# Linear attention stage with a rewritten scalar order and a freed LayerNorm bank, and a 4-bit FFN stage with a reordered TensorE order

## The chip, the cores and the metric

The kernel is written directly against the five engines of a NeuronCore of a Trainium2 chip: TensorE (PE), VectorE (DVE), ScalarE (ACT), GpSimd (POOL) and SyncE (SP). It runs on one core. Every engine has its own program and runs it strictly in the order written; the programs meet at semaphores. The metric is the device time of one execution in microseconds, as the median of several runs.

## What is computed

The reference is a chain of twelve stages on an activation `x` of 16 sequences x 256 tokens x 128 channels, all fp32. Four blocks follow one another, each of the form "half an FFN, attention, half an FFN": ffn0, attn0, ffn0, ffn1, attn1, ffn1, ffn2, attn2, ffn2, ffn3, attn3, ffn3. Each stage normalises `x` over the channels and adds its result to `x`. The change touches two of the stage types.

attn1 is eight layers of linear attention with an MLP (H*K = 1024 = 8 blocks of 128 rows, MLP width F = 512 = 4 blocks):

```python
for i in range(8):
    residual = x
    Q  = elu(x @ Wq[i] + bq[i]) + 1
    Kf = elu(x @ Wk[i] + bk[i]) + 1
    V  = x @ Wv[i] + bv[i]
    KV, sumK = sum_over_tokens(Kf * V), sum_over_tokens(Kf)
    att = Q * KV * (1 / (Q * sumK + 1e-6))
    y = gelu(att @ Wo[i] + bo[i])
    x = layer_norm(y + residual) * s1 + b1
    residual = x
    h = gelu(x @ W1[i] + c1[i])
    h = gelu(h @ W2[i] + c2[i])
    x = layer_norm(h + residual) * s2 + b2
```

ffn3 (which runs twice) quantises to 4-bit floats and back, in blocks of 16 along the last dimension:

```python
h = silu(fp4(x) @ fp4(w_gate).T) * (fp4(x) @ fp4(w_up).T)     # 352 columns
out = fp4(h) @ fp4(w_down).T
```

## The kernel before

**Tiling.** The 4096 tokens are taken in G = 8 groups of GT = 512 tokens (QT = 4 tiles of 128). All of `x` stays in SBUF. PSUM is one tensor `bank` of 8 banks of 128 x 512 fp32. Scratch of every stage lies in one SBUF tensor, `arena`, so most rows of the profile name only `arena` and `bank` and must be told apart by their lines.

**Software pipeline.** A stage is a list of parts (lag, function) for each engine. Slot s calls each part for group s - lag, in the order of the list. `over_groups` runs the 8 slots of an ordinary stage and the slots of its tail. `over_layers` runs attn1: eight layers of eight slots, 64 in all, and 3 slots of tail; group g of layer l + 1 starts where group 7 of layer l has only begun, so that the pipeline does not drain between layers. The loop over the layers is a loop on the chip, at whose edge every engine branches.

**attn1.** `steps(layer)` writes the four lists by hand. It goes through w = 0..7, the eight blocks of 128 rows of a projection. The lists before, for PE, block by block (lag in brackets):

- w0: `proj_pe(0)` [0], `turn_in_pe(0)` [2], `h2_pe(2)` [3], `out_pe(4)` [1]
- w1: `proj_pe(1)`, `h2_pe(3)` [3], `out_pe(5)` [1]
- w2: `proj_pe(2)`, `turn_back_pe(0)` [2], `out_pe(6)` [1]
- w3: `proj_pe(3)`, `out_pe(7)` [1]
- w4: `proj_pe(4)`, `h_pe` of MLP block 0 [2]
- w5: `proj_pe(5)`, `h_pe` of MLP blocks 1, 2, 3 [2], `turn_in_pe(1)` [3], `out_pe(0)`, `out_pe(1)`
- w6: `proj_pe(6)`, `turn_back_pe(1)` [3], `h2_pe(0)` [2], `out_pe(2)`
- w7: `proj_pe(7)`, `h2_pe(1)` [2], `out_pe(3)`

`proj_pe(i)` (L1805) makes three 128 x 512 products, k, q and v of block i, into a ring of five banks (`RING1` = 2, 3, 4, 5, 7); product m waits until product m - 5 has been read. Each fp32 product is two passes of TensorE, so it shows as two MATMULs. `out_pe` (L1820) accumulates att @ Wo in bank 6. `h_pe` (L1849) makes the four blocks of the MLP's inner layer in banks `HBANK` = (0, 1, 6, 0). `h2_pe` (L1859) accumulates the second MLP product in bank 1. `turn_in_pe(i)` (L1876) and `turn_back_pe(i)` (L1885) are the four 128 x 128 transposes into and out of token-major form that LayerNorm i (0 or 1) needs; both use bank 0.

ACT, block by block: `exp_act(w)` (L1896 exp of k, L1897 relu of k, L1900 exp of q), then `inv_act` (L1909 Ln, L1912 Exp), of block w - 2, except that w4 has none and w5 has blocks 2 and 3. After `norm_act(0)` (L2034) in w1 and `back_act(0)` (L1952) in w2 comes the gelu phase in w4: load the gelu table (L1917), `h2_act` (L1939, reads bank 1), `y_act` (L1923, reads bank 6), `h_act` for the four MLP blocks (L1932), load the exp table (L1943). `norm_act(1)` (L2034) ends w5, `back_act(1)` (L1956) ends w6.

DVE, block by block: `feature_dve(w)` (L1968 to L1986; it reads the q and v banks), `att_dve(w - 3)` (L2009), with `norm_stats_dve(0)` (L2020, L2025) at the end of w0 and `norm_stats_dve(1)` at the end of w4. POOL: `query_pool(w)` (L2046), `ratio_pool(w)` (L1997), the residual additions and the rstd of both LayerNorms (L2068 to L2075) after the stats.

**ffn3.** DVE, per slot: `stats_dve` [0], `apply_dve` [1], `quant_x_dve` [1], `quant_h_dve` [2], `add_dve` (L852) [3]. The quantisation is `fp4_steps`, ten DVE instructions (L705 to L714), on 512 elements per partition for x and on 1408 for h. `quant_h_dve` first makes four products silu x up (L811), each for one tile q of 352 columns, straight from the PSUM bank. PE: `transpose_pe` (L784) [0], `down_pe` (L831 transposes, L837 products) [1], `up_pe` (L794 gate, L795 up) [0]; `up_pe` for tile q waits until L811 has read the banks of tile q - 2. ACT: `copy_act` (L336) [0], `copy_h_act` (L847) [1], `silu_act` (L804) [0].

Of the kernel before, what the change touches and what calls it, by code (L numbers as in the profile page):

```python
# [10 lines left out]
ALU = mybir.AluOpType  # L11
# [3 lines left out]
P = 128  # L15
# [23 lines left out]

ARENA = 28320  # L40

# [127 lines left out]
def macaron(nc, A, out, stages=STAGES):  # L169
    ctx = ExitStack()  # L170
    with ctx:
# [546 lines left out]
        if "ffn3" in used:  # L718
# [18 lines left out]
            f3_h = scratch("f3_h", [P, QT, FF3])  # L737
            f3_silu = scratch("f3_silu", [P, 2, FF3])
            f3_xq = scratch("f3_xq", [P, 2, QT, D])
# [5 lines left out]
            f3_up = ev("f3_up", per=QT)  # L745
            f3_act = ev("f3_act", per=QT)
            f3_mul = ev("f3_mul", per=QT, credit=2, by="vector")
            f3_turned = ev("f3_turned", per=len(F3B), credit=2 * len(F3B), by="tensor")
# [16 lines left out]
        def ffn3(n, rep):  # L765
# [21 lines left out]
            def up_pe(g, u):  # L787
                s = g + rep * G
                xt_ready.wait(nc.tensor, g + n * G)
                if n and isinstance(g, int) and g == 0:  # L790
                    x_written.wait(nc.tensor, n * G - 1)
                for q in range(QT):
                    f3_mul.wait_free(nc.tensor, s, q + 1)
                    nc.tensor.matmul(bank[:, 2 + 2 * (q % 2), 0:FF3], xT_tile(u, q), wgT[:], start=True, stop=True)  # L794
                    nc.tensor.matmul(bank[:, 3 + 2 * (q % 2), 0:FF3], xT_tile(u, q), wuT[:], start=True, stop=True)\  # L795
                        .then_inc(f3_up.sem, 1)

            def silu_act(g, u):
                s = g + rep * G
                if n and isinstance(g, int) and g == 0:  # L800
                    x_written.wait(nc.scalar, n * G - 1)
                for q in range(QT):
                    f3_up.wait(nc.scalar, s, q + 1)
                    nc.scalar.activation(f3_silu[:, q % 2, :], bank[:, 2 + 2 * (q % 2), 0:FF3], ACT.Silu)\  # L804
                        .then_inc(f3_act.sem, 1)

            def quant_h_dve(g, u):
                s = g + rep * G
                for q in range(QT):
                    f3_act.wait(nc.vector, s, q + 1)  # L810
                    nc.vector.tensor_tensor(f3_h[:, q, :], f3_silu[:, q % 2, :], bank[:, 3 + 2 * (q % 2), 0:FF3],  # L811
                                            ALU.mult).then_inc(f3_mul.sem, 1)
                f3_mul.wait(nc.vector, s)
# [36 lines left out]
            def add_dve(g, u):  # L850
# [7 lines left out]
            programs["tensor"].append(lambda e: over_groups(  # L858
                e, [(0, transpose_pe), (1, down_pe), (0, up_pe)], gate(e, n)))
            programs["scalar"].append(lambda e: over_groups(  # L860
                e, [(0, copy_act), (1, copy_h_act), (0, silu_act)], gate(e, n)))


# [785 lines left out]
        if "attn1" in used:  # L1649
# [76 lines left out]
            RING1 = (2, 3, 4, 5, 7)  # L1726
            HBANK = (0, 1, 6, 0)

        def attn1(n, rep):
# [54 lines left out]
            def steps(layer):  # L1784
# [5 lines left out]

                def proj_pe(i):
                    def fn(g, u):
# [5 lines left out]
                        if i % 4 == 0 and isinstance(g, int):  # L1798
                            nc.tensor.wait_ge((a1_half0, a1_half1)[i // 4], 48 * (layer + 1))
                        for j, k in enumerate("kqv"):  # L1800
                            m = 3 * i + j

# [28 lines left out]
                def h_pe(blocks):  # L1831
                    def fn(g, u):
                        t = turn(g)
                        for i in blocks:
# [12 lines left out]
                            if i == 3:  # L1847
                                a1_h_act.wait(nc.tensor, t, 1)
                            nc.tensor.matmul(bank[:, HBANK[i], :], w1a[:, i * P:(i + 1) * P], a1_x1[:, u, :],  # L1849
# [15 lines left out]
                def turn_in_pe(i):  # L1865
                    def fn(g, u):
                        t = turn(g)
                        lns[i]["in"].wait(nc.tensor, t)
                        if i == 0:
                            a1_zt.wait(nc.tensor, t - 2)  # L1870
                            if first_layer and g + 2 < G:
                                xt_ready.wait(nc.tensor, n * G + g + 2)
                        elif not (isinstance(g, int) and g == G - 1):
                            a1_h_act.wait(nc.tensor, t + 1)
                        for q in range(QT):
# [209 lines left out]
                for w in range(NB1):  # L2085
                    pe.append((0, proj_pe(w)))
                    if w == 0:
# [9 lines left out]
                    if w == 5:  # L2097
                        pe += [(2, h_pe((1, 2, 3))), (3, turn_in_pe(1))]
                        of(pe, out_pe, 0)
                    if w == 6:  # L2100
                        pe += [(3, turn_back_pe(1)), (2, h2_pe(0))]
                    if w == 7:
                        pe.append((2, h2_pe(1)))
                    if w != 4:
# [5 lines left out]
                    if w == 5:  # L2110
                        of(act, inv_act, 2)
                    if w != 4:
                        of(act, inv_act, w - 2)
                    if w == 1:
                        act.append((2, norm_act(0)))
                    if w == 2:
                        act.append((2, back_act(0)))
                    if w == 5:
                        act.append((3, norm_act(1)))
                    if w == 3 and first_layer:  # L2120
                        act.append((-1, first_act))
                    if w == 6:
                        act.append((3, back_act(1)))

                    dve.append((0, feature_dve(w)))
# [816 lines left out]
```

## Time and profile before

| what | value |
|---|---|
| time, median of 3 runs (lowest to highest) | 5036.86 us (5023.66 to 5044.8) |
| the profiled execution | 5024.43 us, of which the span of the core's instructions is 5022.6 us |
| PE busy | 4048.0 us, 81% of the span |
| DVE busy | 3528.2 us, 70% |
| ACT busy | 3069.5 us, 61% |
| POOL busy | 1550.1 us, 31% |
| attn1's 64 slots of projections | 746.8 to 3363.9 us |
| the two ffn3 stages | about 3835 to 4078 and 4786 to 5023 us |

The page also cuts the span into 40 slices and gives the busy tenths of every engine:

```profile
PE   4487759999989999998998999983877549999944
...
DVE  4588569877777777777777777765657745666576
ACT  1355328888888888888888888881221115565511
...
PEclk9678679999999999999999999996998669999976
```

A digit is the busy share of a slice of 125.6 us in tenths; PEclk is TensorE's granted clock in tenths of full speed. The long stretch of nines and eights from the seventh slice on is attn1. The last slices of each row are the second ffn3.

### The profile page before, as it was taken

The page shows a single profiled execution, that of the slowest core. Times are in us where ns is not written, and L with a number is a line of the kernel's source. Part 1 is how long each engine was busy: PE and PEld are TensorE (multiplying, and loading weights), DVE is VectorE, ACT ScalarE, POOL GpSimd, SP SyncE. Part 2 cuts the span into 40 slices and gives each one's busy share as a digit, 9 for nine tenths or more (in the row PEclk, how much of TensorE's full clock was granted, in tenths as well). Part 3 has the DMA queues.
Part 4 walks back from the last instruction along what each step waited for, and adds up shares of the span by engine and source line. Part 5 has one row for each costly group of instructions (what it writes and reads, how often), then busy time and mean ns, then how long its engine had stood idle before and what let it go on. Part 6 is the DMA issues. An engine that isn't in the chain of part 4 may idle for free.

```text
span 5022.6 us, 66047 instructions
## 1 busy us (share of the span) xinstructions
PE 4048.0 (81%) x15980; PEld 2267.0 (45%) x15980; DVE 3528.2 (70%) x11356; ACT 3069.5 (61%) x5586; POOL 1550.1 (31%) x2846
## 2 busy tenths in 40 slices
PE   4487759999989999998998999983877549999944
PEld 2265633444444444443443444432554436676633
DVE  4588569877777777777777777765657745666576
ACT  1355328888888888888888888881221115565511
POOL 1222124444434444343443443432100023333300
PEclk9678679999999999999999999996998669999976
DMA  1011010000000000000000000000000001111000
GB/s 52 17 32 22 15 21 1 1 20 3 12 12 1 18 5 1 20 3 14 9 1 18 5 6 17 1 1 0 0 0 0 0 22 42 40 40 39 26 0 17
DMA packets 132031, 69.71 MB, mean 14 GB/s; under 512 B 92345, under 2 KB 124814, under 8 KB 129316
## 3 DMA queue, kind: packets, MB, share of 16 engines
q1 hardware_dynamic: 124020, 52.62, 4.3%
q10 hardware_dynamic: 7600, 12.58, 0.7%
q8 instruction: 139, 2.28, 0.2%
q14 instruction: 272, 2.23, 0.1%
HBM read 52.39 MB, written 12.80 MB: 13 GB/s over the span
## 4 chain that ended last, share of the span: by engine, by line
PE 46%; DVE 19%; ACT 15%; issue 11%; POOL 4%; DMA 3%; ACTq 1%; SPq 1%; DVEq 0%; POOLq 0%
PE bank L1805 11%; PE bank L1849 4%; PE bank L1820 4%; PE bank L2574 3%; ACT arena L2034 3%; ACT arena L1909 3%; PE bank L1859 3%; DVE arena L2009 2%; DMA packed_dram<-arena 2%; DVE arena L1986 2%; ACT arena L1897 2%; PE bank L2607 2%; ACT arena L1900 2%; PE bank L643 2%; ACT arena L1896 2%
## 5 line engine op out<-in xcount | busy, mean ns | idle before, releaser
L1805 PE MATMUL bank<-arena 128*128 128x512 f32 x3072 | 1411.0, 596 | 12.1 <-issue 11.8
L1805 PEld LDWEIGHTS bank<-arena 128*128 128x128 f32 x3072 | 588.7, 192 | 761.5 <-issue 749.2
L2046 POOL TENSOR_SCALAR arena<-arena 128x256 f32<-128x256 f32 x1024 | 496.0, 494 | 1215.9 <-DVE arena L1979 1214.8
L1968 DVE SCALAR_TENSOR_TENSOR arena<-arena 128x256 f32<-128x256 f32 x1024 | 393.1, 420 | 303.1 <-ACT arena L1897 303.0
L1820 PE MATMUL bank<-arena 128*128 128x512 f32 x1024 | 537.4, 617 | 39.1 <-DVE arena L2009 38.9
L2009 DVE SCALAR_TENSOR_TENSOR arena<-arena 128x256 f32<-128x256 f32 x1024 | 528.3, 554 | 0.0
L1896 ACT ACTIVATE arena<-bank,bqk 128x512 f32<-128x512 f32 x512 | 351.9, 687 | 221.6 <-PE bank L1805 189.4
L1986 DVE SCALAR_TENSOR_TENSOR arena<-bank,bv,arena 128x256 f32<-128x256 f32 x1024 | 444.7, 472 | 0.0
L1979 DVE SCALAR_TENSOR_TENSOR arena<-bank,bq,arena 128x512 f32<-128x512 f32 x512 | 384.0, 750 | 18.0
L1909 ACT ACTIVATE arena<-arena,const_table 128x512 f32<-128x512 f32 x512 | 374.9, 732 | 0.0
L2585 DVE TENSOR_REDUCE arena<-bank 128x2 f32<-128x512 f32 x256 | 176.2, 688 | 258.5 <-PE bank L2576 258.3
L1900 ACT ACTIVATE arena<-bank,bqk 128x512 f32<-128x512 f32 x512 | 355.9, 695 | 0.7 <-PE bank L1805 0.7
L1897 ACT ACTIVATE arena<-bank,bqk 128x512 f32<-128x512 f32 x512 | 351.5, 686 | 0.0
L1912 ACT ACTIVATE arena<-arena 128x512 f32<-128x512 f32 x512 | 322.5, 630 | 16.3
L2561 POOL TENSOR_TENSOR arena<-arena 128x256 f32<-128x256 f32 x256 | 185.9, 726 | 439.7 <-DVE arena L2551 439.1
L2618 ACT ACTIVATE arena<-bank 128x512 f32<-128x512 f32 x256 | 153.3, 599 | 269.9 <-PE bank L2607 211.1
L2574 PE MATMUL bank<-const_table,arena 128*128 128x256 f32 x1024 | 310.7, 397 | 3.5 <-POOL arena L2561 3.5
L2020 DVE BATCH_NORM_STATS2 arena<-bank 128x6 f32<-128x128 f32 x512 | 113.1, 280 | 280.3 <-PE bank L1876 280.3
L1820 PEld LDWEIGHTS bank<-arena 128*128 128x128 f32 x1024 | 185.5, 197 | 260.1 <-issue 160.7
L1859 PE MATMUL bank<-arena 128*128 128x512 f32 x512 | 284.8, 642 | 0.0
L313 POOL TENSOR_SCALAR rstd<-meanvar 128x4 f32<-128x4 f32 x96 | 20.5, 213 | 782.0 <-DVE meanvar L307 731.8
L1849 PE MATMUL bank<-arena 128*128 128x512 f32 x512 | 244.5, 601 | 1.0 <-ACT arena L1952 1.0
(371 smaller groups left out, 7577.8 us busy)
## 6 DMA issues: line engine op xcount, KB each, us to landing
arena<-packed_dram SPq DMA_DIRECT2D x48, 192.0 KB
arena<-packed_dram ACTq DMA_DIRECT2D x16, 576.0 KB
arena<-diag_dram SPq DMA_DIRECT2D x16, 256.0 KB, 3.9
arena<-in_L_attn_Wk_dram SPq DMA_DIRECT2D x16, 256.0 KB, 3.2
arena<-in_L_attn_Wq_dram SPq DMA_DIRECT2D x16, 256.0 KB, 4.0
arena<-in_L_attn_Wv_dram SPq DMA_DIRECT2D x16, 256.0 KB, 4.4
arena<-in_L_attn_Wo_dram SPq DMA_DIRECT2D x8, 512.0 KB, 3.8
arena<-in_L_attn_W_dram SPq DMA_DIRECT2D x16, 256.0 KB, 2.7
```

What stands on the lines that cost most here:

```text
L1805: nc.tensor.matmul(bank[:, RING1[m % 5], :], w1p[k][:, i * P:(i + 1) * P], zT_of(g), start=True, stop=True).then_inc(a1_proj.sem, 1)
L1820: nc.tensor.matmul(bank[:, 6, :], wo1[:, i, :], a1_att[:, i % 4, :], start=(i == 0), stop=(i == NB1 - 1)).then_inc(a1_outd.sem, 1)
L1849: nc.tensor.matmul(bank[:, HBANK[i], :], w1a[:, i * P:(i + 1) * P], a1_x1[:, u, :], start=True, stop=True).then_inc(a1_h_psum.sem, 1)
L1859: one = nc.tensor.matmul(bank[:, 1, :], w1b[:, i, :], a1_h[:, i, :], start=(i == 0), stop=(i == NF1 - 1))
L1896: nc.scalar.activation(a1_ek[:, i % 4, :], k, ACT.Exp, bias=bqk[:, 0, i:i + 1])
L1897: nc.scalar.activation(a1_kf[:, i % 4, :], k, ACT.Relu, bias=bqk[:, 0, i:i + 1])\
L1900: nc.scalar.activation(a1_eq[:, i % 4, :], q, ACT.Exp, bias=bqk[:, 1, i:i + 1])\
L1909: nc.scalar.activation(a1_z[:, i % 4, :], a1_qf[:, i % 4, :], ACT.Ln, bias=table[:, C_TINY:C_TINY + 1]).then_inc(a1_ln.sem, 1)
L1986: last = nc.vector.scalar_tensor_tensor(seqs(a1_ek[:, i % 4, :])[q], seqs(b[2])[q], bv1[:, i:i + 1], seqs(a1_kf[:, i % 4, :])[q], ALU.add, ...
L2009: last = nc.vector.scalar_tensor_tensor(seqs(a1_att[:, i % 4, :])[q], seqs(a1_qf[:, i % 4, :])[q], a1_kv[:, i % 4, q:q + 1], seqs(a1_z[:, ...
L2046: last = nc.gpsimd.tensor_scalar(a, a, 1.0, a1_ksum[:, i % 4, b:b + 1], ALU.add, ALU.mult)
L2574: nc.tensor.matmul(dst, a3_R[:, w % 4, i * P:(i + 1) * P], table[:, C_KEYS:C_KEYS + T], start=True, stop=False)
```

## The change

In attn1: (a) MLP block 3 goes into bank 1 and no longer into bank 0, its product now waits for the gelu of MLP block 1 (before: of block 0), and `turn_in_pe(1)` waits for the gelu of MLP block 0 alone (before: of all four). (b) `proj_pe(5)` is split: k, then MLP blocks 1 to 3, then q and v, then `turn_in_pe(1)`. (c) `turn_back_pe(1)` moves from behind the products of w6 to behind those of w7. (d) On ACT, `inv_act(3)` moves from w5 to w6, behind `exp_act(6)`; `norm_act(1)` follows it, ahead of `inv_act(4)`; `back_act(1)` moves to w7, ahead of `inv_act(5)`.

In ffn3: (e) PE and ACT do the up products and their silu ahead of the down products of the group before. (f) ACT copies the up product out of PSUM beside the silu, for all four tiles, into double buffers; PE waits for ACT's copy and not for DVE. (g) DVE multiplies silu x up in one instruction of 1408 elements. The arena is 64 elements per partition smaller.

```diff
@@ -37,7 +37,7 @@
 
-ARENA = 28320
+ARENA = 28256
 
@@ -735,7 +735,8 @@
     f3_h = scratch("f3_h", [P, QT, FF3])
-    f3_silu = scratch("f3_silu", [P, 2, FF3])
+    f3_silu = scratch("f3_silu", [P, 2, QT, FF3])
+    f3_upc = scratch("f3_upc", [P, 2, QT, FF3])
     f3_xq = scratch("f3_xq", [P, 2, QT, D])
@@ -743,8 +744,8 @@
     f3_up = ev("f3_up", per=QT)
-    f3_act = ev("f3_act", per=QT)
-    f3_mul = ev("f3_mul", per=QT, credit=2, by="vector")
+    f3_act = ev("f3_act", per=QT, credit=2, by="scalar")
+    f3_mul = ev("f3_mul", credit=2, by="vector")
     f3_turned = ev("f3_turned", per=len(F3B), credit=2 * len(F3B), by="tensor")
@@ -790,7 +791,7 @@
         for q in range(QT):
-            f3_mul.wait_free(nc.tensor, s, q + 1)
+            f3_act.wait_free(nc.tensor, s, q + 1)
             nc.tensor.matmul(bank[:, 2 + 2 * (q % 2), 0:FF3], xT_tile(u, q), wgT[:], start=True, stop=True)
@@ -799,17 +800,18 @@
             x_written.wait(nc.scalar, n * G - 1)
+        f3_mul.wait_free(nc.scalar, s)
         for q in range(QT):
             f3_up.wait(nc.scalar, s, q + 1)
-            nc.scalar.activation(f3_silu[:, q % 2, :], bank[:, 2 + 2 * (q % 2), 0:FF3], ACT.Silu)\
+            nc.scalar.activation(f3_silu[:, u, q, :], bank[:, 2 + 2 * (q % 2), 0:FF3], ACT.Silu)
+            nc.scalar.activation(f3_upc[:, u, q, :], bank[:, 3 + 2 * (q % 2), 0:FF3], ACT.Copy)\
                 .then_inc(f3_act.sem, 1)
...
         s = g + rep * G
-        for q in range(QT):
-            f3_act.wait(nc.vector, s, q + 1)
-            nc.vector.tensor_tensor(f3_h[:, q, :], f3_silu[:, q % 2, :], bank[:, 3 + 2 * (q % 2), 0:FF3],
-                                    ALU.mult).then_inc(f3_mul.sem, 1)
+        f3_act.wait(nc.vector, s)
+        nc.vector.tensor_tensor(f3_h[:], f3_silu[:, u, :, :], f3_upc[:, u, :, :], ALU.mult)\
+            .then_inc(f3_mul.sem, 1)
         f3_mul.wait(nc.vector, s)
@@ -856,9 +858,9 @@
     programs["tensor"].append(lambda e: over_groups(
-        e, [(0, transpose_pe), (1, down_pe), (0, up_pe)], gate(e, n)))
+        e, [(0, transpose_pe), (0, up_pe), (1, down_pe)], gate(e, n)))
     programs["scalar"].append(lambda e: over_groups(
-        e, [(0, copy_act), (1, copy_h_act), (0, silu_act)], gate(e, n)))
+        e, [(0, copy_act), (0, silu_act), (1, copy_h_act)], gate(e, n)))
 
@@ -1724,7 +1726,7 @@
     RING1 = (2, 3, 4, 5, 7)
-    HBANK = (0, 1, 6, 0)
+    HBANK = (0, 1, 6, 1)
 
@@ -1788,7 +1790,7 @@
 
-        def proj_pe(i):
+        def proj_pe(i, which="kqv"):
             def fn(g, u):
@@ -1797,8 +1799,8 @@
                     nc.tensor.wait_ge((a1_half0, a1_half1)[i // 4], 48 * (layer + 1))
-                for j, k in enumerate("kqv"):
-                    m = 3 * i + j
+                for k in which:
+                    m = 3 * i + "kqv".index(k)
 
@@ -1845,7 +1847,7 @@
                     if i == 3:
-                        a1_h_act.wait(nc.tensor, t, 1)
+                        a1_h_act.wait(nc.tensor, t, 2)
                     nc.tensor.matmul(bank[:, HBANK[i], :], w1a[:, i * P:(i + 1) * P], a1_x1[:, u, :],
@@ -1871,7 +1873,7 @@
                 elif not (isinstance(g, int) and g == G - 1):
-                    a1_h_act.wait(nc.tensor, t + 1)
+                    a1_h_act.wait(nc.tensor, t + 1, 1)
                 for q in range(QT):
@@ -2083,7 +2085,7 @@
         for w in range(NB1):
-            pe.append((0, proj_pe(w)))
+            pe.append((0, proj_pe(w, "k" if w == 5 else "kqv")))
             if w == 0:
@@ -2095,12 +2097,12 @@
             if w == 5:
-                pe += [(2, h_pe((1, 2, 3))), (3, turn_in_pe(1))]
+                pe += [(2, h_pe((1, 2, 3))), (0, proj_pe(5, "qv")), (3, turn_in_pe(1))]
                 of(pe, out_pe, 0)
             if w == 6:
-                pe += [(3, turn_back_pe(1)), (2, h2_pe(0))]
+                pe.append((2, h2_pe(0)))
             if w == 7:
-                pe.append((2, h2_pe(1)))
+                pe += [(3, turn_back_pe(1)), (2, h2_pe(1))]
             if w != 4:
@@ -2109,19 +2111,19 @@
                 of(act, inv_act, 2)
-            if w != 4:
+            if w == 6:
+                of(act, inv_act, 3)
+                act.append((3, norm_act(1)))
+            if w == 7:
+                act.append((3, back_act(1)))
+            if w not in (4, 5):
                 of(act, inv_act, w - 2)
...
                 act.append((2, back_act(0)))
-            if w == 5:
-                act.append((3, norm_act(1)))
             if w == 3 and first_layer:
                 act.append((-1, first_act))
-            if w == 6:
-                act.append((3, back_act(1)))
-
             dve.append((0, feature_dve(w)))
```

## Rows read from the trace of the kernel before

**Rows 1.** busy time by stretch: us; busy PE, PEld, DVE, ACT, POOL; clock, DMA.

```profile
746.00:3420.00 2674.00, 2420.54 (x6164) 1082.51 (x6164) 2040.65 (x7761) 2258.07 (x3765) 1072.05 (x2184) 0.98 0.03 8
...
3835.00:4078.00 243.00, 112.32 (x453) 86.03 (x451) 170.14 (x305) 35.01 (x65) 18.87 (x19) 0.68 0.00 0
```

**Rows 2.** waits of PE in attn1: us in total, times, longest us.

```profile
PE bank L1885 <- ACT arena L2034: 145.2, 67, 5.1
PE bank L1876 <- ACT arena L1932: 46.2, 59, 0.9
PE bank L1820 <- DVE arena L2009: 38.9, 64, 2.7
```

**Rows 3.** timeline of PE, one slot: start us, length us; idle and releaser in brackets.

```profile
2000.58 2.74 PE L1805 MATMUL bank<-arena 128*128 128x512 f32 x6
...
2013.48 2.74 PE L1805 MATMUL bank<-arena 128*128 128x512 f32 x6
2016.72 1.13 PE L1820 MATMUL bank<-arena 128*128 128x512 f32 x2 [0.50 <-DVE arena L2009]
...
2021.12 2.74 PE L1805 MATMUL bank<-arena 128*128 128x512 f32 x6
2023.69 2.74 PE L1849 MATMUL bank<-arena 128*128 128x512 f32 x6
2027.21 0.65 PE L1876 MATMUL bank<-const_table,arena 128*128 128x128 f32 x4 [0.78 <-ACT arena L1932]
...
2034.30 0.66 PE L1885 MATMUL bank<-const_table,arena 128*128 128x128 f32 x4 [2.14 <-ACT arena L2034]
...
2043.09 0.69 PE L1805 MATMUL bank<-arena 128*128 128x512 f32 x1 [2.12 <-issue]
```

**Rows 4.** busy time by stretch, two neighbouring slots of attn1.

```profile
2085.21:2127.11 41.90, 38.48 (x97) 17.29 (x96) 31.82 (x122) 35.27 (x62) 16.66 (x34) 0.96 0.02 7
2127.11:2167.34 40.23, 36.79 (x97) 16.52 (x96) 31.51 (x121) 34.94 (x60) 16.70 (x34) 1.00 0.03 8
```

**Rows 5.** timeline of ACT in the slot of rows 3.

```profile
2001.72 0.69 ACT L1896 ACTIVATE arena<-bank,bqk 128x512 f32<-128x512 f32 x1 [1.18 <-PE bank L1805]
...
2018.82 0.69 ACT L1896 ACTIVATE arena<-bank,bqk 128x512 f32<-128x512 f32 x1 [0.38 <-PE bank L1805]
...
2021.98 0.69 ACT L1939 ACTIVATE arena<-bank,bd 128x512 f32<-128x512 f32 x1
...
2024.75 0.69 ACT L1932 ACTIVATE arena<-bank,b 128x512 f32<-128x512 f32 x1 [0.93 <-PE bank L1849]
...
2028.47 0.69 ACT L1896 ACTIVATE arena<-bank,bqk 128x512 f32<-128x512 f32 x1
...
2030.19 0.73 ACT L1909 ACTIVATE arena<-arena,const_table 128x512 f32<-128x512 f32 x1
...
2032.76 1.49 ACT L2034 ACTIVATE arena<-bank,arena 128x128 f32<-128x128 f32 x4
...
2040.29 0.63 ACT L1912 ACTIVATE arena<-arena 128x512 f32<-128x512 f32 x1
```

**Rows 6.** timeline of DVE behind the second LayerNorm's stats, same slot.

```profile
2029.77 0.43 DVE L1968 SCALAR_TENSOR_TENSOR arena<-arena 128x256 f32<-128x256 f32 x1 [0.44 <-ACT arena L1897]
...
2032.45 1.04 DVE L2009 SCALAR_TENSOR_TENSOR arena<-arena 128x256 f32<-128x256 f32 x2
```

**Rows 7.** who waited for ffn3's silu, line L804, both stages.

```profile
L804 ACT ACTIVATE arena<-bank x64: 463/463/464, 3851.5 to 4991.6; 128x352 f32<-128x352 f32 x64
L804 ACT ACT_TABLE_LOAD  x2: 1283/1283/1283, 3850.2 to 4796.7; - x2
...
  DVE arena L811: 92.0, 60
```

**Rows 8.** groups of instructions by line, DVE, first ffn3 stage: busy us, mean ns.

```profile
L811 DVE TENSOR_TENSOR arena<-arena,bank 128x352 f32<-128x352 f32 x32 | 16.6, 521 | 47.1 <-ACT arena L804 47.1
L709 DVE TENSOR_TENSOR arena<-arena 128x1408 f32<-128x1408 f32 x8 | 13.0, 1625 | 0.3
```

## The prediction

> **What bounds the kernel now.** I read the busy time by stretch first. attn1 takes 2674 us, more than half of the span, and both changed stages are visible in it: in attn1 PE is busy 2420.54 us, so nothing can go fast there that does not free PE; in a ffn3 stage DVE is busy 170.14 of 243 us and PE 112.32 [rows 1]. Then the timeline of PE over one attn1 slot, where the reader is to see how the slot is filled: a block of three products starts at 2021.12 and what follows it at 2023.69, so a product streams in 2.57 / 3 = 0.857 us, and between blocks nothing is lost except in three places [rows 3]. By the starts they cost 16.72 - (13.48 + 2.57) = 0.67 us in front of the last product of att @ Wo, 27.21 - (23.69 + 2.57) = 0.95 in front of `turn_in_pe(1)`, and the idle 2.14 + 0.17 = 2.31 in front of `turn_back_pe(1)` (0.17 is what the starts show beyond the idle time in the other two). An undisturbed slot is 40.23 us [rows 4], so PE's own stream with its small change is 40.23 - 3.93 = 36.3 us, of which about 0.2 is weight loads that the three stalls leave bare: 36.1. The three stalls run through the stage: 67, 59 and 64 times [rows 2].
>
> A fourth loss follows the third. The slot at 2085.21 has the same three stalls and takes 41.90 us at a mean granted clock of 0.96, its neighbour 40.23 at 1.00 [rows 4]: 0.04 x 2 x 41.9 = 3.4 us at the lower of the two levels (1.2 instead of 2.4 GHz), and 1.67 us lost. In the timeline the lower level comes straight after the 2.31 us stall when it comes, not after the other two. The stage's mean clock of 0.98 [rows 1] is 0.02 x 2 x 2674 = 107 us at the lower level, about 30 such stretches. A fifth, 2.12 us of issue at a layer's edge [rows 3], comes once a layer and the change leaves it alone.
>
> ffn3 is DVE's: what it waits for there is `silu_act`, 92.0 us over both stages [rows 7].
>
> **The change part by part.**
>
> Steps (c) and (d), the LayerNorm's way back. `norm_act(1)` is what the 2.31 us wait ends on. Now PE first does the products of w6, `h2_pe(0)`, `out_pe(2)` and those of w7. I walk the slot of rows 3 again with the new order. It is unchanged up to 2021.12.
>
> Step (b), the gelu phase. k of block 5 streams until 21.98. MLP block 1 goes to bank 1, which `h2_act` frees at 21.98 + 0.69 = 22.67 [rows 5]; PE starts it at 22.72, a new stall of 0.74 plus 0.1 for a bare weight load (the row at 2016.72 is 1.13 long). Before, the three products of block 5 lay over that wait. From a product's start to its gelu is 24.75 - 23.69 = 1.06 us, so the gelus of MLP blocks 1 and 2 start at about 23.88 and 24.74.
>
> Step (a), bank 1 for MLP block 3. It waits for the gelu of block 1, 23.88 + 0.69 = 24.57, where PE would be ready at 24.54: 0.08 plus 0.1. It starts at 24.62, its gelu at 25.78, where it was at 26.47 (the last of four gelus at the pace of the products). So everything on ACT behind the gelu phase is 0.69 us earlier: `exp_act(5)` at 27.78, not 28.47 [rows 5]. PE does q and v of block 5 until 27.29 and goes on to `turn_in_pe(1)` without waiting, 0.08 later than before. The 0.95 stall is gone, for 1.02 of new ones.
>
> Then w5 to w7. ACT: an exp block is 30.19 - 28.47 = 1.72, and exp plus two inversions 32.76 - 28.47 = 4.29, so an inversion is 1.29 [rows 5]. `norm_act(1)` now starts at 27.78 + 2 x 1.72 + 2 x 1.29 = 33.8 and ends at 35.3. PE: `turn_in_pe(1)` 0.43, two products 1.71, block 6 2.57 and `h2_pe(0)` 0.86 bring it to 32.87, where `out_pe(2)` needs att(2). DVE ran feature(5) and att(2) from 29.77 to 33.49, after 0.44 of waiting for ACT [rows 6]; the relu is earlier now but the stats are not, so from about 29.4 to 33.12: a new stall of 0.30 plus 0.1. Block 7 then streams until 36.7, and `turn_back_pe(1)` finds the norm done 1.4 us before. What hides its chain is exactly the 2.57 + 0.86 + 0.86 + 2.57 that now lies ahead of it; 2.31 goes to 0. The slot ends at 36.7 + 0.43 + 1.72 = 38.85.
>
> What is late next is ACT. From 2028.47 to the end at 2040.92 it never stood still [rows 5], and the new order holds the same instructions: 12.39 us from `exp_act(5)` to where `exp_act(0)` could start, now 27.78 + 12.39 = 40.17. PE has k of block 0 ready 1.14 us (01.72 - 00.58) after its slot begins, at 39.99. ACT, which waited 1.18 us there [rows 5], is now 0.18 behind. That passes through feature(0), the first LayerNorm's stats and norm and att(7) to PE's wait in w3: 0.85 plus 0.1. In w4 ACT waits for PE again (0.38 [rows 5]), so the lag does not add up from slot to slot.
>
> New slot: 36.1 + 0.84 + 0.18 + 0.40 + 0.95 = 38.47 us, 1.76 less than 40.23. Layers 1 to 7 are 56 slots and the first layer has 5 with all lags: 61 x 1.76 = 107 us. Slots that fill or drain the pipeline I take at nothing; waiting for a second gelu could cost the three tail slots some 0.7 each.
>
> The clock. With no stall over 1 us outside the layer edges, I take all but seven to nine of the 30 low stretches as gone: 21 x 1.67 = 35 us. Its bounds are 0 and 50.
>
> By the Trainium skill (TensorE: Matmul & The Clock Gate, HAM oscillation), what puts the clock back is an idle gap longer than any that this slot has; by that rule the 2.31 us stall is not the cause and the 35 us stay. The trace speaks against it, since the drops follow that stall. It is the second rival below.
>
> Steps (e), (f), (g), ffn3. PE does the up products while DVE still quantises the group before, with most of a group's DVE work (170.14 / 8 = 21 us [rows 1]) still ahead, so the 92.0 us of waiting [rows 7] go, except in the first group of each stage, where nothing lies ahead. Four products of 0.521 become one of 1408 elements from SBUF; the same size and kind takes 1.625 [rows 8]: 64 x 0.52 - 16 x 1.66 = 6.6 us less. ACT's 64 added copies are of the silu's size, 0.463 each [rows 7], 15 us a stage on an engine busy 35 of 243 us [rows 1], hidden behind DVE. In the first group DVE now waits for all four tiles behind the table load (1.283 [rows 7]), which eats what that group's one instruction saves, some 2.6 us a stage. Sum 92.0 + 6.6 - 5.3 = 93 us. What hides the moved work is DVE's quantising of h in the group before; DVE, nearly unbroken, is the bound then. (The smaller arena moves nothing in time.)
>
> **Sum.** 107 + 35 + 93 = 235 us off the profiled execution's 5024.43: 4789. That execution lies 12.4 us below the median of 5036.86, so I give 4802 for the median, rounded to 4800.
>
> **The rivals.** First, ACT becomes the bound in attn1. Its work in a slot is 34.9 us of 40.2 [rows 4], 2 to 3 us short of the new slot, and it waits at the gelu phase by construction. If one more such wait is not covered, each us of it is a us of the slot: at 1 us, 61 us in all, 4861. For it: the 0.18 us lag. Against: 0.38 of idle in w4, and more in w0 and w1.
>
> Second, the low stretches stay: 35 us, 4835.
>
> Third, ffn3 gives only part: if PE still reached the up products late, the single multiply would wait for all four tiles instead of the first. Half the gain lost is 47 us, 4847. Against: PE is idle more than half of that stage.
>
> Fourth, faster than forecast: the stalls of w3 and of `out_pe(2)` do not appear because DVE's gaps close up as well, 0.95 + 0.40 over 61 slots, 82 us at most; half of it, 4760.
>
> Fifth, slower than before. The place is bank 1: it now carries MLP blocks 1 and 3 and the second product's sum, so `h_pe` of block 1 stands in PE's strict order waiting for `h2_act`, with q and v of block 5 behind it, which DVE's feature(5) needs. If ACT reached the gelu phase late by x, PE would stand x, hand it to DVE and ACT, and get it back. It decides once x exceeds 235 / 61 = 3.9 us a slot; at 5 us the time would be 4800 + 61 x 5 = 5105. Against: ACT's start of w4 is set by PE's own products, and it had idle time there.
>
> **How the numbers follow.** Forecast 60%; ACT bound 14%; clock stays 8%; ffn3 partly 5%; faster still 10%; slower than before 3%. The range: the bounds of the clock (0 to 50 us), of the new stalls (0.3 us a slot either way, 18 us), the first group, and the run-to-run spread of 21 us give 4765 to 4840 around the forecast; taking in the rivals above up to 61 us, 4750 to 4868. About 0.5% (25 us) is what a measurement of this kernel can tell from no change; all but the fifth case lie beyond it: faster 0.96, same 0.01, slower 0.03.
>
> **What would show it.** In the profile after: slots of 38.3 to 38.7 us between the first products; no wait of L1885 on L2034 in full slots; a wait of about 0.7 us in front of the first L1849 of w5, on L1939; L1820 in w3 at 0.8 to 0.9; low clock stretches at layer edges alone; DVE in ffn3 with next to no wait on L804, groups some 5.5 us shorter. Wrong would be a slot over 39.2 us with ACT idle under 2 us (first rival), a PEclk of 0.98 in attn1 (second), or one wait on L804 per group in ffn3 (third).

## The result, and the profile after

The changed kernel takes 4803.35 us (median of 4 runs, 4797.98 to 4810.98) against 5037.62 us (4 runs, 5023.66 to 5044.8): the ratio is 0.9536 with a 95% interval of 0.9509 to 0.9563, 234 us less. The forecast was 4800. The profiled execution took 4797.98 us. Two lines were added above attn1's code, so attn1's lines of the profile are two higher than before: L1807 are the products of the projections, L1822 `out_pe`, L1851 `h_pe`, L1878 `turn_in_pe`, L1887 `turn_back_pe`, L2011 `att_dve`, L2036 `norm_act`, L1941 `h2_act`; in ffn3 L806 is the silu, L807 the copy and L813 the multiply.

By stretch, with the columns of rows 1 (the first line is attn1 from the first product of a projection to the last, the others are the two ffn3 stages):

```profile
755.00:3240.00 2485.00, 2363.91 (x6079) 1038.40 (x6080) 2019.29 (x7706) 2221.28 (x3719) 1063.59 (x2161) 1.00 0.04 8
3719.00:3895.00 176.00, 110.34 (x447) 82.80 (x445) 155.95 (x242) 46.44 (x97) 8.07 (x13) 0.74 0.00 0
4612.00:4796.00 184.00, 109.02 (x448) 81.70 (x448) 156.07 (x242) 46.32 (x97) 7.86 (x12) 0.74 0.04 12
```

Against rows 1, attn1's mean clock is 1.00 for 0.98, and DVE is busy 156 of 176 us in ffn3 for 170 of 243 (that window is wider than the stage). Taken from the same instructions in both traces, the 226.4 us between the two spans (5022.6 and 4796.2) divide like this:

| part of the span | before | after | difference |
|---|---|---|---|
| stages ahead of attn1's first product | 746.8 | 755.3 | +8.5 |
| attn1, first to last product of a projection | 2617.2 | 2484.8 | -132.4 |
| from there to the first ffn3's up products | 483.5 | 480.2 | -3.3 |
| first ffn3, up products to last addition | 221.0 | 173.8 | -47.2 |
| attn3, up to the second ffn3's up products | 725.5 | 719.6 | -5.9 |
| second ffn3, to the end | 228.7 | 182.5 | -46.2 |

The waits of PE in attn1 answer rows 2:

```profile
PE bank L1822 <- DVE arena L2011: 58.3, 72, 2.8
PE bank L1851 <- ACT arena L1941: 35.2, 61, 0.6
PE bank L1887 <- ACT arena L2036: 32.9, 31, 5.1
```

`turn_back_pe` fell from 145.2 us to 32.9; what is left is in the tail (18.1 us) and in `turn_back_pe(0)`, mostly behind the layer edges, and `turn_back_pe(1)` waits for nothing in any full slot; `turn_in_pe(1)` no longer waits for the gelus at all; new is MLP block 1 waiting for `h2_act`, 35.2 us in 61 slots. The timeline of PE over one slot (start us, length us, idle and releaser in brackets) answers rows 3:

```profile
1910.31 2.74 PE L1807 MATMUL bank<-arena 128*128 128x512 f32 x6
...
1926.65 1.12 PE L1822 MATMUL bank<-arena 128*128 128x512 f32 x2 [0.71 <-DVE arena L2011]
...
1931.05 1.02 PE L1807 MATMUL bank<-arena 128*128 128x512 f32 x2
1932.65 3.03 PE L1851 MATMUL bank<-arena 128*128 128x512 f32 x6 [0.58 <-ACT arena L1941]
1935.52 1.88 PE L1807 MATMUL bank<-arena 128*128 128x512 f32 x4
1937.23 0.60 PE L1878 MATMUL bank<-const_table,arena 128*128 128x128 f32 x4
...
1939.39 2.74 PE L1807 MATMUL bank<-arena 128*128 128x512 f32 x6
...
1943.03 1.13 PE L1822 MATMUL bank<-arena 128*128 128x512 f32 x2
```

The products of block 0 start at 1910.31 and those of the next group 38.41 us later, for 40.23 in rows 4. This is a slot away from the layer edges, as are all slots named below by one length; in a layer of eight, the two beside the edge and the three after them are longer (see the layer's edge). The reader is to see the wait in w3 (1926.65), k of block 5 alone at 1931.05, the wait for `h2_act` at 1932.65, q and v at 1935.52, and that the transposes at 1937.23 and everything behind them come without a gap; `turn_back_pe(1)` has no idle time in its row any more.

### The profile page after: what moved, and what is told of

Same layout as the page of the kernel before. It is cut to its first block, busy times and chain, and to the rows that moved or that the text cites. A ratio compares the mean times of both kernels' runs of the same rounds, so it can differ in the third digit from the quotient of the medians.

```text
span 4796.2 us, 66046 instructions
## 1 busy us (share of the span) xinstructions
PE 4027.6 (84%) x15980; PEld 2235.2 (47%) x15980; DVE 3511.9 (73%) x11308; ACT 3084.9 (64%) x5650; POOL 1555.8 (32%) x2846
## 4 chain that ended last, share of the span: by engine, by line
PE 44%; DVE 20%; ACT 15%; issue 12%; DMA 3%; POOL 3%; ACTq 1%; SPq 1%; DVEq 0%; POOLq 0%
PE bank L1807 11%; PE bank L1822 6%; PE bank L1851 4%; PE bank L2576 4%; ACT arena L1902 3%; DMA packed_dram<-arena 2%; PE bank L1861 2%; ACT arena L1911 2%; ACT arena L2036 2%; DVE arena L2011 2%; ACT arena L1898 2%; PE bank L643 2%; PE bank L2609 2%; ACT arena L1899 2%; DVE arena L1988 2%
## 5 line engine op out<-in xcount | busy, mean ns | idle before, releaser
L1807 PE MATMUL bank<-arena 128*128 128x512 f32 x3072 | 1416.0, 594 | 12.8 <-DVE arena L1988 11.6
L1807 PEld LDWEIGHTS bank<-arena 128*128 128x128 f32 x3072 | 584.3, 190 | 751.7 <-issue 726.7
L2048 POOL TENSOR_SCALAR arena<-arena 128x256 f32<-128x256 f32 x1024 | 511.8, 510 | 1079.3 <-DVE arena L1981 1076.9
L1822 PE MATMUL bank<-arena 128*128 128x512 f32 x1024 | 528.9, 608 | 59.6 <-DVE arena L2011 58.3
L2011 DVE SCALAR_TENSOR_TENSOR arena<-arena 128x256 f32<-128x256 f32 x1024 | 530.7, 557 | 0.0
L1822 PEld LDWEIGHTS bank<-arena 128*128 128x128 f32 x1024 | 173.7, 190 | 290.2 <-DVE arena L2011 172.6
L1851 PE MATMUL bank<-arena 128*128 128x512 f32 x512 | 260.8, 622 | 36.1 <-ACT arena L1941 35.2
```

The costliest lines, as they stand in the source:

```text
L1807: nc.tensor.matmul(bank[:, RING1[m % 5], :], w1p[k][:, i * P:(i + 1) * P], zT_of(g), start=True, stop=True).then_inc(a1_proj.sem, 1)
L1822: nc.tensor.matmul(bank[:, 6, :], wo1[:, i, :], a1_att[:, i % 4, :], start=(i == 0), stop=(i == NB1 - 1)).then_inc(a1_outd.sem, 1)
L2011: last = nc.vector.scalar_tensor_tensor(seqs(a1_att[:, i % 4, :])[q], seqs(a1_qf[:, i % 4, :])[q], a1_kv[:, i % 4, q:q + 1], seqs(a1_z[:, ...
L2048: last = nc.gpsimd.tensor_scalar(a, a, 1.0, a1_ksum[:, i % 4, b:b + 1], ALU.add, ALU.mult)
```

## Experiments

Each kernel was run beside the kernel before. Where a total rests on a single execution, the table of stages and the slots are what the verdict goes by: attn3 alone, which no kernel here touches, took 719.6 to 744.9 us from one profiled execution to another, on the whole the longer the more of it was at the low clock (some 99 us of 719.6, 137 us of 744.9; 38 us more at half the clock account for at most 19 of these 25).

**The two parts by themselves.** `attn_only` is the changed kernel with ffn3 as before, `ffn_only` the reverse.

> The attn1 part of the change alone; ffn3 as before. My theory: the two parts lie in stages that don't overlap, so the gains add. attn1's slots 38.4 us as with the whole change, no low clock stretch inside attn1, and the whole 93 us of ffn3 missing: about 4897 us, 2.8% under before. Rival (a part of the attn1 gain came from the smaller activity of the other stage, or from the place of the scratch in memory): outside 4885 to 4910.

> The ffn3 part alone; attn1 as before, with slots of 40.23 and 41.9 us and some 28 low clock stretches. My theory: 5037.6 less 93 to 94 us, about 4944 us, 1.9% under before; DVE in ffn3 waits for the silu only in the first group of each stage. If the gains of the two parts didn't add, this and attn_only together would differ from the whole change's 234 us by over 15 us.

Measured: 4905.91 us (4 runs; ratio 0.9752, 0.9722 to 0.9781) and 4940.95 us (4 runs; 0.9821, 0.9791 to 0.9851), beside 5035.49 us. The gains are 129.6 and 94.5 us and add to 224.1, where the whole change gave 234 against its own runs of the kernel before: within the 15 us set. In the traces the parts separate cleanly: attn1 takes 2486.9 us in the one and 2619.8 in the other, the two ffn3 stages 221.9 + 229.4 and 173.8 + 182.6. The parts are independent within what these runs can tell. One thing forecast for `attn_only` did not come: attn1 has three low clock stretches there, all at layer edges, where the changed kernel has none with the same attn1.

**The way back too early.** `early_back` undoes step (c) alone:

```diff
                     if w == 6:
-                        pe.append((2, h2_pe(0)))
+                        pe += [(3, turn_back_pe(1)), (2, h2_pe(0))]
                     if w == 7:
-                        pe += [(3, turn_back_pe(1)), (2, h2_pe(1))]
+                        pe.append((2, h2_pe(1)))
```

> The whole change, but turn_back_pe(1) again ahead of the products of w6's tail, as before (ACT keeps its new order). PE reaches it at about 2032.0 on the clock of the walked slot, the norm ends at 2035.3: a stall of 3.3 us in every slot, slot 41.2 us without clock losses (the stall in front of out_pe(2) goes). Theory A (the low clock stretches follow long stalls of PE): they come back, in at least half of the slots, mean granted clock in attn1 0.95 to 0.98, total about 5025 to 5075 us. Rival B (the low stretches have another cause and went for another reason): clock 1.00 in attn1, slots of 41.2 us, total about 4975 us.

Measured: 5061.82 us (one execution), 258 us over the changed kernel and slower than the kernel before. The timeline of PE behind the stall, and the stretch from 800 to 3190 us with the columns of rows 1:

```profile
2004.03 1.11 PE L1887 MATMUL bank<-const_table,arena 128*128 128x128 f32 x4 [3.16 <-ACT arena L2036]
2004.94 1.91 PE L1861 MATMUL bank<-arena 128*128 128x512 f32 x2
...
2008.35 3.52 PE L1807 MATMUL bank<-arena 128*128 128x512 f32 x6
```

```profile
800.00:3190.00 2390.00, 2139.94 (x5278) 946.18 (x5277) 1741.71 (x6648) 1935.74 (x3223) 922.48 (x1869) 0.95 0.04 8
```

The stall is 3.16 us by the row and 3.33 by the starts, as walked. A pair of passes that takes 1.02 us takes 1.91 after it, three products 3.52 for 2.74, and the mean clock in attn1 is 0.95. Slots without a low stretch are 41.3 us (forecast 41.2), the median slot 42.99. Theory A holds, rival B falls.

**(a) and (b) without (c) and (d), and the reverse.** `ab_only` puts `turn_back_pe(1)`, `norm_act(1)`, `back_act(1)` and `inv_act(3)` where they were. `cd_only` takes bank 0 for MLP block 3 again, with its old waits, and does not split block 5:

```diff
-            HBANK = (0, 1, 6, 1)
+            HBANK = (0, 1, 6, 0)
...
-                    pe.append((0, proj_pe(w, "k" if w == 5 else "kqv")))
+                    pe.append((0, proj_pe(w)))
...
-                        pe += [(2, h_pe((1, 2, 3))), (0, proj_pe(5, "qv")), (3, turn_in_pe(1))]
+                        pe += [(2, h_pe((1, 2, 3))), (3, turn_in_pe(1))]
```

> The new bank, the split block 5 and all of ffn3, but turn_back_pe(1), norm_act(1), back_act(1) and inv_act(3) where they were before. By the walk PE reaches turn_back_pe(1) at 2032.0 and the norm ends at 2033.57: a stall of 1.6 us, slot 39.5 us, so the steps (a) and (b) give 0.75 of the 1.83 us. Theory A of the clock: a stall of 1.6 us is followed by few or no low stretches (those of 0.95 us were not): clock 1.00, total about 4870 us. If stalls of any length over 1 us bring low stretches: 20 or more of them, total over 4900 us.

> The whole change without its steps (a) and (b): MLP block 3 in bank 0 again, block 5 not split. The new place of turn_back_pe(1) and ACT's new order stay. By the walk: the stall in front of turn_in_pe(1) is 0.95 again, turn_back_pe(1) waits for nothing, out_pe(2) waits 0.76 for att(2), ACT is 0.5 us behind at exp_act(0) and PE's wait in w3 grows to 1.2: slot 39.15 us, so (c) and (d) alone give 1.1 of the 1.83 us. No low clock stretches. Total about 4803 + 61 x 0.75 = 4850 us. If (a) and (b) only moved a stall and gave nothing, it would be at 4803.

Measured: 4856.85 us with slots of 39.56 us, and 4850.54 us with slots of 39.08 (one execution each). The stall in the first, and in the second the two in front of `out_pe(7)` and `turn_in_pe(1)`:

```profile
2004.54 0.66 PE L1887 MATMUL bank<-const_table,arena 128*128 128x128 f32 x4 [1.43 <-ACT arena L2036]
```

```profile
1985.62 1.12 PE L1822 MATMUL bank<-arena 128*128 128x512 f32 x2 [0.81 <-DVE arena L2011]
...
1996.11 0.66 PE L1878 MATMUL bank<-const_table,arena 128*128 128x128 f32 x4 [0.78 <-ACT arena L1934]
```

By the starts they are 1.59, 0.97 and 0.94 us, for 1.6, 1.2 and 0.95 walked; a third in the second kernel, in front of `out_pe(2)`, is 0.69 for 0.76. So (a) and (b) alone take 0.67 us off a slot of 40.23, (c) and (d) alone 1.15, and both 1.82: in the slots they add. Over attn1 they do not: by itself the one takes 82.1 us off (2535.1 for 2617.2), the other 87.9 (2529.3), and both 132.4, since either alone already ends the low clock stretches behind the third stall. In full slots neither kernel has a low stretch of the clock; the four that `ab_only` has between 800 and 3190 us, and the one of `cd_only`, all follow a stall of 2.34 to 2.89 us at a layer's edge.

**The layer's edge.** In the changed kernel a layer takes 313.9 us (mean of the six whole layers in the middle, between their first products), and 8 x 38.41 is 307.3, so an edge costs 6.6. The timeline of ACT at an edge:

```profile
1987.93 0.63 ACT L1914 ACTIVATE arena<-arena 128x512 f32<-128x512 f32 x1
1992.01 1.28 ACT L2223 ACT_TABLE_LOAD   x1 [3.45 <-issue]
1993.30 0.21 ACT L2188 ACTIVATE bqk<-cols_qk 128x16 f32 x1
1993.78 0.69 ACT L1898 ACTIVATE arena<-bank,bqk 128x512 f32<-128x512 f32 x1 [0.26 <-ACT bqk L2188]
```

ACT ends its last inversion at 1988.56, does nothing for 3.45 us ("issue", the branch of the loop), loads a table, copies biases and starts on block 0 at 1993.78. `unrolled` writes the layers out and keeps the waits in front of the bias copies; `noload` keeps the loop and drops the table load from it.

```diff
-    with eng.Fori(1, layers) as layer:
+    for layer in range(1, layers):
         one_layer(layer, -G)
...
```

> The whole change with the loop over attn1's layers written out, so that no engine of the four branches at a layer's edge (SyncE's loop stays; the table load and the copies of the biases stay). In the changed kernel eight slots of 38.4 make 307.2 us, and a layer takes 314.4. Theory A: 5 to 6 of these 7.2 us are the branch, above all ACT's 3.45 us of issue there, which ACT has no slack to make up: layers of 309 us, 7 x 5.5 = 38 us less, about 4765 us. Rival B: the edge's cost is in the table load and the bias copies, or the longer program costs issue time of its own: 4795 us or more.

> The whole change, with the loop, but without ACT's load of the exp table at the start of each layer (the table of the last slot is the same one). Theory A: ACT is late at the edge by all that it does there, so 1.28 us come off each of seven layers: 313.1 us each, about 4794 us. Rival: the edge is set by PE's own 2 us of issue, and the load is covered: layers of 314.4 us, 4803.

Measured: layers of 310.3 us (`unrolled`) and 312.6 (`noload`), for 313.9; totals of 4798.22 us (4 runs, 4789.62 to 4807.33) and 4801.32 us (one execution). So the branch, of all engines together, is 3.6 us of an edge's 6.6 and the load 1.3. The load is ACT's alone and counts in full, so ACT's lateness there is not covered; how the 3.6 divide between the engines was not tried, and if the two add, 1.7 of the 6.6 are left that no run took away. Theory A has the mechanism, and its 5.5 us a layer were 1.9 too many. The total of `unrolled` is another matter: attn1 is 23.3 us shorter (2461.5 us), the whole only 5, which by the total alone would speak for rival B. In its profiled execution the 25 us are in attn3 (744.9 for 719.6 us). The last experiment comes back to that.

**ffn3 in halves.** `f3_order` has only the new order (e), with the four multiplies from PSUM; `f3_copy` has only the copies and the one multiply (f, g), with the old order.

> Step (e) alone in ffn3 (with all of attn1's part): the up products ahead of the down products, but four multiplies that read PSUM and no copies. The first two tiles are then ready, the third and fourth wait for PE and ACT behind the first multiply: some 1.2 + 0.7 us of waiting a group for 4.9, none of the 10.8 us in the last group: about 60 of the 93 us. Total about 4836 us. If the copy were what matters, it would be near 4896.

> Steps (f) and (g) alone in ffn3 (with all of attn1's part): copies and one multiply, but the up products behind the down products as before. The multiply then waits for all four tiles of silu and copy instead of the first: from the walk of one group it starts some 5 us behind the end of the quantisation of x and the group takes about 1.3 us more than in the kernel before. A ffn3 stage of 221 and 229 us in the kernel before would take 5 to 15 us more, total about 4896 + 21 = 4917 us. If the copy alone were the gain (it alone frees PE from DVE), the stages would take under 200 us.

Measured (one execution each): 4884.55 us with stages of 208.6 and 219.5 us, and 4888.54 us with stages of 221.4 and 230.7, for 221.0 and 228.7 in the kernel before and 173.8 and 182.5 with both. My figure for the order alone was wrong by a factor of three: it gives 21.6 of 93.4 us, not 60. The copy alone gives nothing, as expected, and costs 2 us rather than 21. The timeline of `f3_order` in one group shows why:

```profile
3805.62 0.95 DVE L811 TENSOR_TENSOR arena<-arena,bank 128x352 f32<-128x352 f32 x2
...
3806.20 1.54 PE L794 MATMUL bank<-wgT,xT 128*128 128x352 f32 x2 [12.04 <-DVE arena L811]
...
3807.53 1.38 PE L795 MATMUL bank<-wuT,xT 128*128 128x352 f32 x2
...
3809.44 0.52 DVE L811 TENSOR_TENSOR arena<-arena,bank 128x352 f32<-128x352 f32 x1 [2.87 <-ACT arena L804]
...
3811.02 0.52 DVE L811 TENSOR_TENSOR arena<-arena,bank 128x352 f32<-128x352 f32 x1 [1.06 <-ACT arena L804]
...
3818.37 0.76 PE L794 MATMUL bank<-wgT,xT 128*128 128x352 f32 x2
```

The first two tiles are multiplied at once. PE then does the third tile, for which it has stood idle 12 us behind DVE's first multiply, and its passes come at half speed (granted clock 0.50 from 3806.2 to 3809.5): 1.54 us for a pair that takes 0.76 at 3818.37. DVE waits 2.87 and 1.06 us here, 3.9 in all, and 4.5 in the mean of the 16 groups. In the kernel before it is 4.9 to 6.5 in most groups and 13.0 in the last one of each stage; some 17 of the 21.6 us come from these two last groups. What the half speed costs shows in the first group of the kernel before, where the first two tiles are ready too and PE does the third at full speed:

```profile
3853.96 0.86 PE L794 MATMUL bank<-wgT,xT 128*128 128x352 f32 x2 [1.49 <-DVE arena L811]
...
3855.94 0.52 DVE L811 TENSOR_TENSOR arena<-arena,bank 128x352 f32<-128x352 f32 x1 [1.61 <-ACT arena L804]
...
3857.12 0.52 DVE L811 TENSOR_TENSOR arena<-arena,bank 128x352 f32<-128x352 f32 x1 [0.66 <-ACT arena L804]
```

That is 2.3 us of waiting for 4.5, so by this comparison, which is an estimate, the clock takes some 2.2 us a group, 35 of the 38 us by which the order alone fell short of my 60. As long as PE needs a bank that DVE frees in the middle of its quantisation, going early only moves the wait. In `f3_copy` the 16 multiplies wait 104.8 us:

```profile
  ACT arena L807: 104.8, 16
```

and in the changed kernel the same line waits only in the first group of each stage:

```profile
L813 DVE TENSOR_TENSOR arena<-arena x16: 1615/1625/1626, 3729.2 to 4764.5; 128x1408 f32<-128x1408 f32 x16
...
  ACT arena L807: 5.6, 2
```

So neither half alone is the gain: 21.6 and -2 us for 93.4. The copy unbinds PE from DVE, the order uses it.

**What bounds the new slot.** `late7` takes the wait in w3 away by doing `out_pe(7)` after the products of block 4; `kq` covers the wait for `h2_act` with one more product of block 5.

```diff
-                    if w != 4:
+                    if w == 4:
+                        pe.insert(-1, (1, out_pe(7)))
+                    elif w != 3:
                         of(pe, out_pe, w - 4)
```

```diff
-                    pe.append((0, proj_pe(w, "k" if w == 5 else "kqv")))
+                    pe.append((0, proj_pe(w, "kq" if w == 5 else "kqv")))
...
-                        pe += [(2, h_pe((1, 2, 3))), (0, proj_pe(5, "qv")), (3, turn_in_pe(1))]
+                        pe += [(2, h_pe((1, 2, 3))), (0, proj_pe(5, "v")), (3, turn_in_pe(1))]
```

> The whole change, with out_pe(7) behind the products of block 4 in w4 instead of those of block 3 in w3, where PE waits 0.87 us for att(7) in every slot. Theory A (ACT is now next to PE as the bound): PE no longer waits there, but ACT can use only the 0.46 us that it idled in front of exp_act(4), and PE's wait in front of MLP block 1 grows from 0.74 to about 1.2 us: slots of 37.95 us, 61 x 0.45 = 27 us less, about 4776 us. Rival B (PE alone is the bound): the 0.87 us and its bare load go whole, slots of 37.4 us, about 4745 us. Rival C: nothing is gained since ACT sets the slot: 4803 us.

> The whole change, with k and q of block 5 ahead of MLP blocks 1 to 3 and only v behind them. This covers PE's 0.74 us wait for h2_act by another product. Theory A (ACT is the bound): MLP block 1 starts 0.1 us later than before, so ACT gains nothing, and what PE gains it gives back in front of out_pe(2) and in w3: slots of 38.3 to 38.4 us, total 4795 to 4805 us. Rival B (PE is the bound): slots of 37.6 us, about 4755 us.

Measured: `late7` 4771.22 us (4 runs; ratio 0.9466, 0.9441 to 0.9490) with slots of 37.95 us; `kq` 4804.55 us (one execution) with slots of 38.41. The waits of PE in attn1, first of `late7`, then of `kq`:

```profile
PE bank L1851 <- ACT arena L1941: 68.5, 61, 1.2
...
PE bank L1822 <- DVE arena L2011: 10.6, 8, 2.8
```

```profile
PE bank L1822 <- DVE arena L2011: 103.9, 131, 2.7
```

`late7` takes 48 us of waiting for DVE away and gets 33 of it back in front of MLP block 1 (68.5 us for 35.2; 1.25 us a slot by the starts for 0.74). `kq` takes those 35.2 us away altogether and pays 45.6 in front of `out_pe` (103.9 for 58.3). PE's stalls can be moved at will now. Only what ACT can use comes off the slot, the 0.46 us that it idled in w3 to w4. Theory A held in both to 0.1 us a slot; PE alone is not the bound any more.

**The best of them.** `late7_unrolled` joins the late product and the written-out layers.

> The two gains together: out_pe(7) in w4, and attn1's layers written out. In attn1 the late product gave 27 us (2484.8 to 2457.8 us of projections) and the written-out layers 23 (2484.8 to 2461.5, 4 us a layer). Theory A (they are independent: one is in every slot, the other at the edges): slots of 37.95 us, layers of 306 to 307 us, attn1 2430 us, and the whole 4803 - 50 = about 4750 us. In the written-out run before, attn3 took 745 us for the 720 to 734 of the others, with 140 us at the low clock there for 99 to 133, so that its total was hardly lower. Theory A takes that as chance: attn3 under 735 us here. Rival B (the longer program costs later stages about 20 us, each time): attn3 740 us or more, total about 4770 us, no better than the late product alone.

Measured: 4759.7 us (5 runs, 4757.8 to 4777.39; ratio 0.9462, 0.9442 to 0.9481), the fastest here: 44 us under the changed kernel and 275 under the kernel before, though only 11.5 under `late7`, with ranges that overlap. Slots are 37.91 us, layers 306.7, attn1 2436.2 us, 21.6 under `late7`: in attn1 the two gains are independent. attn3 took 734.8 us in the profiled execution, inside what other kernels showed (`noload`, which has the loop, 734.3), but it is again at the upper end, and the total lies 10 us over theory A's. Whether the longer program costs attn3 some 10 us or whether both executions met a low clock there by chance stays open: the two ranges of single executions overlap.

## Why the prediction was right, step by step

- **The third stall.** Forecast to go from 2.31 us to nothing: it did, in every full slot. `early_back` shows that the place on PE is the whole of it, the same ACT order with the old place gives 3.3 us.
- **The gelu phase.** Forecast 0.74 us in front of MLP block 1 and 0.08 in front of block 3; 0.74 by the starts, and at most 0.2 in front of block 3. `turn_in_pe(1)` went on without waiting.
- **`out_pe(2)`.** Forecast 0.30 and 0.1: the starts show a wait of 0.21, and the row at 1943.03 has the bare load, 1.13 for 1.02. DVE went from the stats straight to feature(5), some 0.1 us earlier than I had it.
- **ACT next to PE.** Forecast 0.85 in w3 plus 0.1 for the bare load: 0.87 by the starts, and the load. All stalls of the slot together are 2.31 us by the starts for the 2.37 of the sum. The slot came to 38.41 us for 38.47; `late7` and `kq` show that ACT, with the chain it waits in, is indeed what the slot now ends on. The step from 40.23 is 1.82 for 1.76 us, 111 for 107 us over 61 slots; the slots near an edge have more, which is the term below.
- **The clock.** Forecast: 21 of 30 low stretches go, 35 us. There were 28, 95.6 us in all, and none is left between the same points (a first one, at 811 us in the filling of the pipeline, is within the first 60 us that this count leaves out). That is 95.6 / 2 = 48 us. 24 of them followed the third stall and four a stall at a layer's edge. I had kept one for each edge; the other kernels with short stalls show none to four there, so up to 7 us of the 48 is chance. The rule of the Trainium skill (TensorE: Matmul & The Clock Gate, HAM oscillation), by which the drops would not hang on gaps as short as these (2.3 and 3.3 us), came out against the runs: they follow the stall wherever it is put.
- **The layer's edge: the term that was missed.** "A fifth, 2.12 us of issue at a layer's edge, comes once a layer and the change leaves it alone." It does not. ACT's 3.45 us of issue, its table load and its bias copies were there before, under the 1.2 us that ACT idled at block 0 and the time that PE lost itself. With that slack gone the edge costs 6.6 us for 2.9 (before, a layer takes 330.7 us, eight slots of 40.23 are 321.8, and the low clock in it costs 6.0): the slots on its two sides are some 40.5 and 41.6 us in the mean, the next three 38.9. The first edge, into the loop, costs 3.5 for 0.5. The seven are 27 us that the sum did not have. `unrolled` and `noload` give back 3.6 and 1.3 of the 6.6.
- **Sum of attn1.** 111 + 48 - 27 = 132, and 132.4 us measured, for 142 forecast. It is near because a clock term too small by 13 us stood against one of 27 that was missing. With ffn3 the two parts gave 225.8 us for the 235 of the sum, and the profiled executions differ by 226, the medians by 234: that 4803 lies so near to 4800 is in part luck.
- **ffn3.** 93.4 us for 93 (its term of 6.6 for the multiplies is 6.7 by its own figures). The first groups wait for all four tiles, 5.6 us in both stages together, of the 92.0 in [rows 7]. The mechanism behind it I had not understood as well as the sum suggests: the order alone gives 23% of it and not the 64% that I expected, and the copy alone nothing.
- **Rivals.** ACT as the bound was right as a description and wrong as a price: it does not add a microsecond, it takes away from what could be had, and `late7` got 0.46 us a slot of that. The 34.9 us of ACT's work lie 3.6 us short of the forecast slot, not 2 to 3. The fifth rival, slower than before, did not come about in the changed kernel; a kernel slower than before is reached at once by moving `turn_back_pe(1)` alone (`early_back`), through a stall and the clock behind it.

## What to carry to other kernels

When two engines are both within 10% of a slot, walk one slot on the rows with the order of each queue; it gave the slots of six kernels here to 0.1 us, though single stalls in them only to 0.2. Price the rare places (loop edges, first and last groups) by each engine's slack there and not by what the bound engine shows today, since slack is what such a change spends. And for a handover through PSUM, ask which engine frees the bank: a new order was worth little until a copy let the idle engine free it.

## What was not expected of the hardware

The clock's drops go with the length of PE's stall. In every kernel here, each stretch at 1.2 GHz between 800 and 3190 us came right after a stall of 2.1 us or more by the starts. Not every such stall had one: in that window 49 stretches (228.7 us) came after 53 stalls of 3.15 to 3.33 us (`early_back`), 22 after 56 of 2.1 to 2.31 us (the kernel before, which has four more after stalls at layer edges), and none in full slots after stalls of 1.59 us and of 0.9 (`ab_only`, `cd_only`). Each stretch after a 2.31 us stall cost 1.67 us, three quarters of the stall again. A shorter stall thus returned more than its own length: the third stall was 140 us over the stage, the clock behind it 41.
